# A quantised linear layer in three float32r products per product: wider seven-product columns, one more mixed pair, and the order of VectorE's steps around them

## The reference

```
w_eff = quantised(weight + lora_delta, scale, codebook) * scale + lora_delta      # 2048 x 2048
y     = x @ w_eff.T
out   = x + y @ W_base.T + b_base + 2 * mixed(y @ A_w.T, softmax(y @ router_w.T), cores) @ B_w.T
```

## Time and profile before

| | |
|---|---|
| median of 3 runs | 2318.55 us (2316.69 to 2319.56) |
| profiled execution | 2317.91 us, span 2316.1 us |
| TensorE matmul busy | 2240.4 us (97%), 11610 matmuls |
| TensorE weight load busy | 2022.0 us (87%) |
| VectorE busy | 1969.0 us (85%) |
| ScalarE busy | 1496.5 us (65%) |
| GpSimd busy | 1381.3 us (60%) |
| DMA | 56.7% of 16 engines, 198 GB/s |
| chain that ended last | 85% TensorE, 9% VectorE, 3% ScalarE |

### The profile page before, as it was taken

How to read it: one execution, slowest core, us unless ns; L and a number is a source line. 1 busy time by engine, 2 the same in 40 slices (tenths; PEclk the granted TensorE clock), 3 DMA queues, 4 the chain that set the end, 5 groups by cost and what they waited for, 6 DMA issues and landing times.

```text
span 2316.1 us, 31908 instructions
## 1 busy us (share of the span) xinstructions
PE 2240.4 (97%) x11610; PEld 2022.0 (87%) x11610; DVE 1969.0 (85%) x2509; ACT 1496.5 (65%) x1962; POOL 1381.3 (60%) x894
## 2 busy tenths in 40 slices
PE   3889899999999999999999999999999999999999
PEld 2445479999999989899999989899999999999998
DVE  8999998889997977999997988999996766777776
ACT  7999978989886765666664865666663664122121
POOL 6888846669874534888775635887872132333231
PEclk9999999999999999999999999999999999999999
DMA  5787855444434434666664334666656666646554
GB/s 208 261 287 274 313 211 178 163 147 156 149 129 141 116 109 177 234 239 248 246 229 156 116 105 173 226 247 253 248 211 201 186 189 186 240 190 229 194 218 155
DMA packets 133234, 459.63 MB, mean 198 GB/s; under 512 B 14114, under 2 KB 66914, under 8 KB 96354
## 3 DMA queue, kind: packets, MB, share of 16 engines
q1 hardware_dynamic: 133076, 457.59, 56.7%
HBM read 306.41 MB, written 151.13 MB: 198 GB/s over the span
## 4 chain that ended last, share of the span: by engine, by line
PE 85%; DVE 9%; ACT 3%; DMA 1%; issue 1%; POOL 0%; DVEq 0%; SPq 0%; POOLq 0%; ACTq 0%
PE m L1239 6%; PE m L1238 6%; PE m L1240 6%; DVE acc L1713 6%; PE m L1190 5%; PE m L1192 5%; PE m L1191 5%; PE m L1296 4%; PE m L1298 4%; PE m L1297 4%; PE m L1346 4%; PE m L1348 4%; PE m L1347 4%; PE m L1131 4%; PE m L1307 3%; PE m L1306 3%
## 5 line engine op out<-in xcount | busy, mean ns | idle before, releaser
L1713 DVE SCALAR_TENSOR_TENSOR acc<-mk,dj,acc 128x1024 f32<-128x1024 uint8 x736 | 943.2, 1282 | 66.3 <-ACT mk L1461 47.9
L1461 ACT ACTIVATE mk<-wr,bj 128x1024 uint8<-128x1024 f32 x736 | 811.7, 1140 | 3.0 <-DVE acc L1713 2.1
L2034 POOL TENSOR_TENSOR pp<-pp,tm 128x1024 f32<-128x1024 f32 x184 | 454.0, 2468 | 22.3 <-POOL tm L2020 0.6
L2020 POOL TENSOR_SCALAR tm<-mp,dj 128x1024 f32<-128x1024 uint8 x192 | 226.0, 1178 | 211.0 <-ACT mp L1467 203.5
L1817 DVE TENSOR_TENSOR kl<-kw,kh 128x416 fp32r<-128x416 f32 (+3 forms) x310 | 237.6, 775 | 85.8 <-ACT kh L1496 84.7
L1496 ACT ACTIVATE kh<-kw 128x416 fp32r<-128x416 f32 (+3 forms) x310 | 169.1, 548 | 182.1 <-DMA kw<-in_wb 91.8
L1239 PE MATMUL m<-gl,xh 128*128 128x384 f32 (+2 forms) x800 | 280.9, 351 | 0.0
L1238 PE MATMUL m<-gh,xh 128*128 128x384 f32 (+2 forms) x800 | 280.6, 351 | 0.0
L1240 PE MATMUL m<-gh,xl 128*128 128x384 f32 (+2 forms) x800 | 279.8, 350 | 0.0
L1467 ACT ACTIVATE mp<-wr,bj 128x1024 uint8<-128x1024 f32 x224 | 255.1, 1139 | 0.0
L1773 DVE TENSOR_TENSOR part<-m,part 128x512 f32<-128x512 f32 (+4 forms) x362 | 217.6, 610 | 30.9 <-PE m L1240 16.6
(11 more groups left out here) (249 smaller groups left out, 5169.8 us busy)
## 6 DMA issues: line engine op xcount, KB each, us to landing
part<-part SPq DMA_DIRECT2D x191, 1036.0 KB, 4.8
rows<-in_wb SPq DMA_DIRECT2D x61, 1036.0 KB, 4.8
out<-part SPq DMA_DIRECT2D x31, 1024.0 KB, 4.8
kw<-in_ws SPq DMA_DIRECT2D x128, 208.0 KB, 2.7
xw<-in_x SPq DMA_DIRECT2D x96, 256.0 KB, 3.3
kw<-in_wb SPq DMA_DIRECT2D x92, 192.0 KB, 2.4
wr<-in_w SPq DMA_DIRECT2D x32, 512.0 KB, 5.9
dl<-delta SPq DMA_DIRECT2D x30, 512.0 KB, 5.3
```

The lines of the kernel that those rows point to most:

```text
L1461: e.activation(R.mk[m % NM], w, ACT.Identity, bias=R.bj[:, j:j + 1], scale=GROW).then_inc(S["mk"], 1)
L1713: e.scalar_tensor_tensor(R.acc, R.mk[m % NM], R.dj[:, j:j + 1], R.acc, ALU.mult, ALU.add).then_inc(S["ac"], 1)
L2034: e.tensor_tensor(R.pp, first, R.tm[scaled_level(q, i)], ALU.add).then_inc(S["pp"], 1)
```

## The change

The seven-product columns grow from 512 to 680 of the 1036 of each half; a product is now 12 matmuls of 340 columns, in two PSUM banks that lie side by side, and the rest is two units of 356 columns a token. The chains take banks m0, m1 and m2, m3; the rest units (u, 0) always m4 and (u, 1) always pd. Pair 15 becomes mixed; pairs 1 and 15 have orders of their own. The operand sums grow from 2 x 512 to 2 x 680 columns; the fourth sum no longer fits beside the others, and is put into G's second block of columns (of blocks 0 and 2), which only the plain pair 0 reads. So its building waits for pair 0's end. Levels in the G stages of groups 1 and 2: 66 each, in the token stages 126 (1 in pair 0, 9 in pairs 1 to 13, 8 in pair 14, none in 15). Within a pair they stand behind the add at all positions but one or two; at position 9, product 4, which `token_sums_low` shares now, there is a level in pairs 7 to 13 and none in pairs 1 to 6 and 14.

```diff
-UNTIL_TOKENS, UNTIL_WEIGHTS = (16, 24, 32), (0, 18.5, 26.5, 32)
+UNTIL_TOKENS, UNTIL_WEIGHTS = (16, 24, 32), (0, 18.75, 26.75, 32)
-GUEST = {4: 2, 5: 0}
-GUEST_LAST = {2: 0, 3: 1, 10: 0, 11: 1}
+GUEST = {1: {4: "x2", 5: "x0"}, 2: {2: "x0", 3: "x1", 4: "x2", 5: "sums"},
+         3: {2: "g0", 3: "g1", 4: "x2", 5: "x0", 10: "g0", 11: "g1"}}
-SW = 512
-REST = (HX - SW) // 3 * 2
-MIX = (("prod", 1), ("prod", 2), ("rest", 0, 0), ("rest", 0, 1), ("prod", 6), ("prod", 5), ("rest", 0, 2), ("prod", 7),
-       ("prod", 3), ("rest", 1, 0), ("prod", 4), ("rest", 1, 1), ("rest", 1, 2))
+SW = 680
+SPLIT_SW, REST = 340, HX - SW
+CHAIN_AT = (512 - SPLIT_SW, 3 * 512 - SPLIT_SW)
+MIX = (("prod", 1), ("prod", 2), ("rest", 0, 0), ("prod", 6), ("prod", 5), ("rest", 0, 1), ("prod", 7), ("prod", 3),
+       ("rest", 1, 0), ("prod", 4), ("rest", 1, 1))
+MIX_START = (("prod", 1), ("prod", 2), ("rest", 0, 0), ("rest", 0, 1), ("prod", 6), ("prod", 5), ("rest", 1, 0), ("prod", 7),
+             ("prod", 3), ("prod", 4), ("rest", 1, 1))
+MIX_END = (("prod", 1), ("prod", 5), ("prod", 6), ("rest", 0, 0), ("prod", 7), ("prod", 3), ("rest", 0, 1), ("prod", 2),
+           ("rest", 1, 0), ("prod", 4), ("rest", 1, 1))
-MIX_FIRST, MIX_LAST = 1, PAIRS - 2
+MIX_FIRST, MIX_LAST = 1, PAIRS - 1
-SPREAD_AT, SPREAD_HIGH_AT = (0, 1, 3), (1, 2, 3, 4)
-SPREAD_LOW, SPREAD_LOW_AT = (2, 0, 1, 3), ((0, 4), (0, 5), (0, 6), (1, 2))
+SPREAD_AT, SPREAD_HIGH_AT = ((0, 0), (0, 2), (1, 0)), ((0, 1), (0, 3), (0, 4), (1, 1))
+SPREAD_LOW, SPREAD_LOW_AT = (0, 1, 2, 3), ((0, 5), (0, 6), (1, 1), (1, 3))
+SPLIT_AT = {1: {5: (0,), 6: (1, 2), 7: (3, 4), 8: (5, 6), 10: (7,)}, 2: {5: (0,), 6: (1,), 7: (2,), 8: (3,)}}
-VECTOR_SPLITS = (17, 19, 21, 23, 25, 27, 28, 29, 30, 31)
+VECTOR_SPLITS = (18, 22, 19, 23, 25, 27, 28, 29, 30, 31)
-WAIT_LEVELS, END_LEVELS, WAIT_SLOTS = 8, 11, 4
+WAIT_LEVELS, END_LEVELS, WAIT_SLOTS = 10, 11, 4
...
-            if at == 7:
+            if at == (6 if mixed(p) else 7):
                 yield ("x_low", g, 2 * p + 3)
-            if at == (11 if mixed(p) else 9) and mixed(p + 1):
+            if at == (MIX_OF[p].index(("prod", 3)) + 2 if mixed(p) else 9):
                 yield ("token_sums_high", g, p + 1)
-                if p:
-                    yield ("token_sums_low", g, p + 1)
-            if (p, at) == (1, 1):
-                yield ("token_sums_low", g, 1)
+                yield ("token_sums_low", g, p + 1)
...
-def unit_bank(u):
+def unit_chain(u):
+    return 1 if u[2] in (2, 3, 5) else 0
+
+
+def unit_banks(u):
     if u[1] == "chunk":
-        return u[3]
+        return {u[3]}
     if u[1] == "prod":
-        return 1 if u[2] in (2, 3, 5) else 0
-    return 2 + (6 * u[0] + 3 * u[2] + u[3]) % 4
+        return {2 * unit_chain(u), 2 * unit_chain(u) + 1}
+    return {NCH - 1 + u[3]}
...
         if kind == "prod":
-            n = at[0]
+            n, first = at[0], CHAIN_AT[unit_chain(UNITS_OF[g][k])]
+            pieces = ((0, SPLIT_SW), (SPLIT_SW, SW))
             for kp in range(2):
                 high, low = sum_factor(g, p, n, kp)
                 oh, ol = sum_operand(n, kp, False), sum_operand(n, kp, True)
-                e.matmul(bank[:, 0:SW], high, oh, start=kp == 0 and n in (1, 2, 5), stop=False, skip_group_check=n in (3, 4, 6, 7))
...
+                for c0, c1 in pieces:
+                    e.matmul(R.mm[:, first + c0:first + c1], high, oh[:, c0:c1], start=kp == 0 and n in (1, 2, 5), stop=False,
+                             skip_group_check=n in (3, 4, 6, 7))
...
         else:
+            e.wait_ge(S["mc"], multiplied(g, PAIR_FIRST[g][MIX_FIRST] - 1))
             rebuilt(3, 1, 0)
```

More of the change, by code:

```diff
@@ L385, in __init__ @@
         self.tmp = self.put("tmp", at_x[0], 1536)
[L386 to L389, removed]
+        assert 48 * SW <= HIGH * H * 4
+        flat = [[grouped(self.put(f"{name}{k}", at_wh + 8 * SW * (3 * place + k), 2 * SW, dtype), 2) for k in range(3)]
+                for name, place, dtype in (("tr", 0, F32), ("th", 0, F32R), ("tf", 1, F32), ("tl", 1, F32R))]
+        self.sum_raw, self.sum_h, self.sum_f, self.sum_l = flat
+        fourth = [both_blocks(t, 0, 1) for t in (self.put("gf", at_first + 4 * NMAX * DX, NMAX * DX), self.gah, self.gal)]
+        for places, at in zip(flat, (0, 1, 0, 2)):
+            places.append(fourth[at])
         self.sf = self.put("sf", at_las, 1024)
@@ L429, in __init__ @@
         self.pd = bank("pd")
-        self.m = [bank(f"m{c}") for c in range(NCH)]
+        self.mm = bank("m", NCH)
+        self.m = [self.mm[:, 512 * c:512 * (c + 1)] for c in range(NCH)]
         self.pz, self.pm, self.second = self.acc[:, 0:128], self.acc[:, 128:256], (self.acc[:, 512:1024], self.acc[:, 0:512])
@@ L437, in token, with ring @@
         return self.fourth[g] if k == 3 else (self.xw[k], self.xl[k], self.xh[k])
[L439 to L446, removed]
+    def ring(self, g, s):
+        kind = GUEST[g].get(s)
+        if kind is None:
+            return self.kw[s % RING], self.kl[s % RING], self.kh[s % RING]
+        if kind == "sums":
+            return self.sums_guest
+        n = int(kind[1])
+        return self.guest[n] if kind[0] == "g" else (self.xw[n], self.xl[n], self.xh[n])
     def put(self, name, at, n, dtype=F32, rows=128):
@@ L524, in first_at_home @@
 def first_at_home(g, s):
-    guests = {**GUEST, **(GUEST_LAST if g == LAST else {})}
-    return s not in guests and all(k in guests for k in range(s % RING, s, RING))
+    return s not in GUEST[g] and all(k in GUEST[g] for k in range(s % RING, s, RING))
 def wait_consumed(e, S, q):
@@ L556, in units_of_stage @@
         if mixed(p):
-            units += [(p, *u) for u in MIX]
+            units += [(p, *u) for u in MIX_OF[p]]
         else:
@@ L603, in prod_unit, with half_done_at, bank_last @@
 def prod_unit(g, p, n):
-    return PAIR_FIRST[g][p] + MIX.index(("prod", n))
+    return PAIR_FIRST[g][p] + MIX_OF[p].index(("prod", n))
+def half_done_at(p):
+    if not mixed(p):
+        return NCH
+    return 1 + max(k for k, u in enumerate(MIX_OF[p]) if unit_tokens((p, *u))[0] == (0,))
+def bank_last(g, v):
+    return max(k for k, u in enumerate(UNITS_OF[g]) if v in unit_banks(u))
 def multiplied(g, k):
@@ L1301, in mul @@
             _, xl, xh = R.token(g, 2 * p + u)
+            bank = (R.m[NCH - 1], R.pd)[i][:, 0:REST]
             for b in range(GROUP[g]):
@@ L1757, in mul_added @@
         t = 2 * p + unit_tokens(UNITS_OF[g][k])[0][0]
-        part, bank = R.part[t % 3], (*R.m, R.pd)[unit_bank(UNITS_OF[g][k])]
+        part = R.part[t % 3]
         if k == first_unit(g, t, 0):
```

108 lines of the change are left out of this document (57 added, 51 removed).

## The result

The changed kernel takes 2355.50 us (median of 4 runs, 2354.41 to 2356.6) against 2318.22 before: a ratio of 1.0161, 95% interval [1.0143, 1.0179], 37 us slower. Forecast: 2331, range 2308 to 2344. The sign was right, the size three times too small, and the time lies outside the range. The profiled execution took 2356.57 us (span 2354.6), 38.5 us of span more than before. (In one experiment, e11, two of four executions were disturbed; its ratio is of the other two, and none of its rows are shown.)

What follows compares the result with a forecast made beforehand. TensorE was taken as the bound, with VectorE, which empties its banks, as runner-up. Per stage -6.0 + 3.2 + 7.1 + 0.5 + 0.8 + 0.6 = +6.2; 2317.9 + 12.4 + 0.6 = 2331 us, range 2308 to 2344.

Steps and rivals of the forecast that it cites:

- The columns: TensorE in each pair: fewer columns, 45,648 for 46,656, at 155 ns per 340-column matmul, save 6.0 us a stage.
- Rival 4: The columns don't bring it: 340-column matmuls go at today's 159 ns, 12 us becomes 3, total 2340; chance 0.04.
- The chain in pairs 7 to 13: Rest add, sl and a level precede product 4's add, delaying the next pair: 21.85 us, not 20.83; 7.1 a stage.
- the sign: Sign that the forecast is right: pairs 7 to 13 start 21.5 to 22.2 us apart.
- rival 1: VectorE hides it: sl at product 4 costs 1.21 us and pair 1 catches up; 2310 named, chance 0.32.
- Pairs 2 to 6 (+0.5) and 14 (+0.8): No level at product 4: an sl over 2.1 us costs 0.1 a pair; in pair 14 a half's last step costs 0.8.
- Pair 1 (+3.2): Wider operand sums put VectorE behind: four TensorE waits, together 5.5 us, before 2.4 and 1.3; extra 3.2 a stage.
- The rest, nearly free: Levels moved to G stages 0.3, splits in pair 15's last six units hidden, part 31's load 0.3: 0.6 a stage.
- Rival 3: G stages turn VectorE-bound besides, through the five extra levels and ring steps (kl): 3 us a stage, 2337; chance 0.07.

Runs made afterwards that it cites:

- e11: Changed kernel with every second mask step of the halves from 16 on adding half the columns, the rest left out of the weights: 2344 us.
- e1: Changed kernel with the low half of the token sums (sl) moved behind the add of product 4 in mixed pairs: 2329.62 us.
- e5: Changed kernel with pair 15's end reordered: first ring steps two units earlier, one split into G slot 1, two splits to the eleventh unit: 2358.12 us.
- e6: Changed kernel with sl behind the add of product 4, no levels in the first 16 units, and e5's edit: 2327.54 us.
- e9: Changed kernel with four of the eight weight splits of pair 15, first mixed stage, moved into slots 0, 2, 4 and 6 of the G stage: 2357.92 us.
- e4: Changed kernel with six quantisation levels of each G stage returned to the token stages: 2361.59 us.
- e3: Changed kernel with no levels in the first 20 units of a token stage, where it was 10: 2348.48 us.
- e7: Changed kernel with e1's edit and no levels in the first 16 units of a token stage: 2325.56 us.
- e12: e7 with every second mask step of the halves from 16 on adding half the columns, the rest left out of the weights: 2316.73 us.
- e10: Changed kernel with high and low parts of the sums behind product 4, no levels in the first 13 units, and e9's edit: 2328.33 us.

## Why the prediction was right and wrong

Forecast of the span: +12.4; measured +38.5. Of the 26 us between, pairs 2 to 14 are 11.8 (20.8 in both stages, forecast 9.0), the two G stages 10.1 (10.7 against 0.6), the pairs 1 5.7 (11.5 against 5.8), and pair 15 and the rest -1.4.

**The columns (-6.0 a stage): right.** 155.5 ns a matmul for 155, 20.87 us a pair for 20.83, 5.5 us for 6.0. Rival 4 is out. The Trainium skill's figure for an isolated gap (TensorE: Matmul & The Clock Gate, Back-to-back issue gap), N/2.4 + 2.5 ns, gives 144 ns at 340 columns; the trace does not agree, and the measurement decides.

**The chain in pairs 7 to 13 (+7.1): right in place and mechanism; that the size came out near is in part luck.** In stage 1 those pairs last 22.03 us on average, forecast 21.85; over 20.87 that is 8.1 us, in stage 2 9.3. But not one of the fourteen lies between the 21.5 and 22.2 that I gave as the sign. Four of the seven in stage 1 last 21.2, with an sl of 1.22 us, as rival 1 had it, and three last 22.9 to 23.4: two with an sl of 2.90 and 3.10, and pair 9 with 1.92, because there the steps between two halves (L1746 and L1735) put VectorE 1.3 us behind the point where my walk has it in step. e1 shows the cause: with sl behind the add, the waits go. Rival 1 falls: sl's median, 1.48, was near the 1.4 from which it was to decide, but in stage 1 its mean was 1.83, and without slack in the chain it is the mean that counts.

**Pairs 2 to 6 (+0.5) and 14 (+0.8): wrong.** They cost 2.7 and 2.0 us over 20.87. I had placed the last step of a half ahead of sl in pair 14 alone; pair 6 has it too, and there, besides, the step releases GpSimd's scaling, which runs against sl and makes it 2.71. I took sl's length and its neighbours as independent; here the neighbour starts the contender. Pair 5 lost 0.7 us, as sl stood 0.81 us idle for its high part from ScalarE, a wait that the prediction has nowhere. In stage 2 pairs 2 to 14 took 2.1 us more than in stage 1; sl took 3.46 us in pair 2 and 2.54 in pair 7 there.

**Pair 1 (+3.2): under-sized.** It rose by 4.8 and 6.7 us with the columns' gain in it, and by 5.1 and 7.0 without. The sum has a slip: 5.5 less the mean of 2.4 and 1.3 is 3.65, not 3.2. The four waits stand where I put them (926.05, 934.09, 937.30, 941.04), and their idle time is 5.5 us in stage 1 and 6.0 in stage 2, for 5.5. It lies otherwise within them: the first is 2.15 and 2.66 us, not 1.0, as half of the twelve steps that build the sums took 2.0 to 2.2 us and I had summed 1.5, and the other three together are shorter than forecast. So the total of the waits was right, and what the term lacked is the half clock, 1.7 us in each of the two pairs 1, and the 0.2 us that each wait costs beyond its idle time.

**"The rest, nearly free" (+0.6): the step that failed worst for its size.** "The splits fall on pair 15's last six units ...: hidden by that pair, which has no level; if not, the first slot of G waits 2 us". It waited 4.5, and 2.4 more went to the clock; the waits on gl within the G stages, 0.84, 0.53, 1.11 and 1.18 us, were the milder part of it. In all +9.0 at the second and +1.7 at the first. I had costed the splits by their count and single durations, VectorE 4 and GpSimd 4, and not as two queues that shut each other out: 11.75 us for GpSimd's four, 4.62 for two ring steps of 0.54. I had also left out that the adds of the last units queue behind them. e5, e6 and e9 show that the work doesn't fit elsewhere as it stands: the wait is split in two or moves into the slots.

**Half clock: absent from the prediction, 7.5 of the 26 us.** (They are counted in the stretches above.) A wait was costed at its length. Behind some waits TensorE ran at 1.2 GHz, and lost 1.7, 2.4, 1.7 and 1.7 us more; the kernel before has no such stretch in these stages. The length of the wait does not tell by itself. Of the eight waits of 1.9 us or more four were followed by it. The same wait of 2.09 us at the end of pair 9 was followed by it in stage 2 and not in stage 1, and the same wait of 2.74 us at the start of the second G stage in e6 and not in e5. What decides it is left open.

**Rival 3** was right in part: VectorE is full in the first G stage, 39.84 and 39.90 of 40 us, and TensorE waits for it, 1.4 us in the first and 2.3 in the second, where 3 each were named; the waits are on gl, not on kl. But e4 does not show that the levels would be better placed in the token stages.

**What stays open.** Of the 37 us, 26 are the chain (e1). Of the other 11, and the 12 that the columns should have given on top, e3, e7 and e12 account for VectorE's backlog (4 to 9 us), and the start of the second G stage for 7, of which e12 still has 6. A version in which GpSimd's splits do not meet the ring steps was not found, nor one with sl cut in smaller steps tried. e5, e6, e9 and e10 moved single steps only. Whether the wider columns can win is therefore open. That e12, with work left out, only draws level speaks against it as the kernel stands.

## What to carry to other kernels

When a change uses the last free bank of PSUM, look first at what the engine that empties the banks does ahead of each add: a side step moved ahead of an add cost 6 us with two units of cover behind it, and 26, with the level that came along, where one was left. Cost a stretch of side work by the pairs of steps that run against each other, not by their count, and ask of each step which contender it releases. Where a step has two lengths, here 1.2 and about 3 us, walk the chain with each of them: the mean came near, and no single pair was like it. When VectorE is 95% busy or more, most of the work moved off one wait turned up at the next; moving it gained 4 us of 16.

## What the runs showed that was not expected

- A wait can cost more than its length. After 4.5 us, matmuls of 384 columns went at 320 ns a step for about 4.9 us, then at 174; the granted clock in that window was 0.54, at the next 1.00.
- Two VectorE steps of 0.54 us each took 4.62 us beside four GpSimd steps that took 11.75, and 4.61 in e12 again.
- An add over two neighbouring PSUM banks (680 columns) took 0.86 us, what the line through the single-bank adds gives.
